# Softmax attention with maxima from the leading halves, four heads at once in row quarters, and one denominator product a head group

## The reference

```python
def _L1_xattn_ref(x, context, w_q, b_q, w_k, b_k, w_v, b_v, w_o, b_o):
    q = x @ w_q + b_q
    k = context @ w_k + b_k
    v = context @ w_v + b_v
    # reshaped to (B, 512, 16 heads, 32)
    scores = jnp.einsum('bqhd,bkhd->bhqk', q, k) * scale
    weights = jax.nn.softmax(scores, axis=-1)
    out = jnp.einsum('bhqk,bkhd->bqhd', weights, v).reshape(B, Lq, D)
    return out @ w_o + b_o
# x = x + _L1_xattn_ref(layernorm(x), ctx, ...)
```

## Time and profile before

| | us |
|---|---|
| median of three runs | 1724.04 |
| lowest, highest | 1719.91, 1727.51 |
| span of the profiled execution | 1727.3 |
| of it, softmax attention, first projection to last output | 629.7 to 1436.5 |
| one batch of it in the middle (905.1 to 999.6) | 94.5 |

### The profile page before, as it was taken

The page is one execution under the profiler, slowest core; times in us unless marked ns, Lnnn a source line. Parts: engine busy times, 40 slices in busy tenths (PEclk is TensorE's granted clock), DMA queues, the critical chain, the costliest instruction groups (busy, mean ns, idle before and its releaser), DMA issues. The chain is left out here.

```text
span 1727.3 us, 29488 instructions
## 1 busy us (share of the span) xinstructions
PE 1589.8 (92%) x8932; PEld 719.8 (42%) x8932; DVE 1226.5 (71%) x1756; ACT 1150.9 (67%) x1895; POOL 1022.9 (59%) x738
## 2 busy tenths in 40 slices
PE   5999878998999977899999999999999978999998
PEld 3545433443444432334444444444443423444443
DVE  4978898997888745676776767676767665665553
ACT  5667599787888744665757666666657567556662
POOL 4776436765678723565657666665756665455452
PEclk9989999999999997999999999999999989999999
DMA  8421000000000122121211212121211200010001
GB/s 309 146 73 32 1 1 1 1 1 1 0 1 1 45 59 81 32 58 25 58 34 36 56 27 57 27 55 32 58 25 40 55 22 28 25 49 24 24 24 49
DMA packets 60463, 72.22 MB, mean 42 GB/s; under 512 B 14416, under 2 KB 40016, under 8 KB 59856
## 3 DMA queue, kind: packets, MB, share of 16 engines
q1 hardware_dynamic: 56944, 62.22, 12.3%
q10 hardware_dynamic: 3424, 8.91, 1.3%
HBM read 37.40 MB, written 8.39 MB: 27 GB/s over the span
## 5 line engine op out<-in xcount | busy, mean ns | idle before, releaser
L1556 DVE TENSOR_REDUCE s_mx<-bank 128x1 f32<-128x512 f32 x512 | 337.3, 685 | 199.8 <-PE bank L1684 193.7
L1443 ACT ACTIVATE s_E<-bank 128x512 f32<-128x512 f32 x512 | 293.9, 595 | 202.5 <-PE bank L1698 177.2
L1342 POOL TENSOR_TENSOR s_E<-s_E 128x1024 f32<-128x1024 f32 x128 | 300.5, 2367 | 125.4 <-PE bank L1706 117.9
L1684 PE MATMUL bank<-s_KA,s_QA 96*128 96x512 f16 x512 | 194.2, 390 | 17.7 <-DMA s_KA<-sm_cx 7.1
L1698 PE MATMUL bank<-s_QA,s_KA 97*128 97x512 f16 x512 | 196.7, 386 | 3.8 <-DMA s_QA<-s_mrow 1.4
L1335 POOL TENSOR_TENSOR sm_cx<-s_qkf,sm_cx 128x512 f16<-128x512 f32 x64 | 76.5, 1195 | 175.6 <-ACT sm_cx L1421 175.4
L1867 POOL TENSOR_TENSOR sm_cx<-m_xf,sm_cx 128x512 f16<-128x512 f32 x60 | 84.1, 1408 | 104.9 <-ACT sm_cx L1909 104.9
L1706 PE MATMUL bank<-s_E,s_V 128*32 128x512 f32 x1024 | 135.6, 602 | 4.3 <-ACT s_E L1443 4.3
L1075 PE MATMUL bank<-sm_zz,w1raw 128*128 128x512 f16 x256 | 100.3, 392 | 31.1 <-DVE sm_cx L962 16.3
L1098 PE MATMUL bank<-f_w2q,w2raw 128*128 128x512 f16 x512 | 122.2, 380 | 0.4 <-ACT w2raw L912 0.4
L772 POOL TENSOR_TENSOR sm_wkv<-sm_wkv,sm_cx 128x511 f32<-128x511 f32 x48 | 66.1, 1378 | 94.2 <-DVE sm_wkv L962 94.1
(11 more groups left out here) (264 smaller groups left out, 4092.1 us busy)
## 6 DMA issues: line engine op xcount, KB each, us to landing
sm_cx<-in_ctx SPq DMA_DIRECT2D x16, 768.0 KB, 4.6
s_QA<-sm_cx SPq DMA_DIRECT2D x384, 32.0 KB, 1.9
s_KA<-sm_cx SPq DMA_DIRECT2D x372, 32.0 KB, 1.9
X<-in_x SPq DMA_DIRECT2D x8, 1024.0 KB, 6.8
out_x<-X SPq DMA_DIRECT2D x8, 1024.0 KB, 4.3
w1raw<-in_w ACTq DMA_DIRECT2D x1, 4096.0 KB, 14.2
w2raw<-in_w ACTq DMA_DIRECT2D x1, 4096.0 KB, 28.7
w1raw<-in_wq SPq DMA_DIRECT2D x1, 1024.0 KB, 5.1
```

Of the source, the lines that this page charges most:

```text
L1342: e.tensor_tensor(into, into, other, ALU.add).then_inc(s_sum.sem, 1)
L1443: e.activation(E[:, SLOT[k] + h, :], SC[u % 2][:, :], ACT.Exp, scale=1.0 / float(np.sqrt(DH)))\
L1556: e.tensor_reduce(mx[:, q, h:h + 1], MX[q % 2][:, :], AX.X, ALU.max).then_inc(s_red.sem, 1)
L1684: e.matmul(MX[k % 2][:, :], QA[0:MROW, m, h, q * P:(q + 1) * P], KA[0:MROW, m, h, :], start=True, stop=True).then_inc(s_mx.sem, 1)
```

## The change

The rest of the kernel is as before; in `softmax_attention` this is different:

- Maxima multiply only the high halves of queries and keys, straight from qkh (now double-buffered) without the stack: 32 rows a head, the four heads in the four row quarters of the array, into four banks. VectorE reduces four banks in one instruction, and one transpose of 16 columns replaces four. The exact scores keep their stacked operands; the row subtracted from them cancels in the division.
- The exponentials of all four key tiles are added up before one product with ones: five additions on GpSimd and one on VectorE a group (key tile 3, heads 2 and 3), instead of four on GpSimd and two products. The product goes to the bank of the numerators (ND), after these were copied, and the inverse into SBUF (RD). It stands in unit 3 of the next step.
- PSUM is dealt out anew: SC two banks, MX four, ND one, R one. Queries, keys, values and outputs all go through R.
- The output product is spread over m = 0 (four pieces), 1 (eight) and 2 (four). The normalising moves from VectorE to ScalarE, with two small instructions on GpSimd (`centre`). QA and KA have three slots for four.
- The units of all work are dealt out anew, and all programs are written out, without loops.

The tables and bank numbers:

```diff
-    NSH = 12
-    SPARSE_K, SPARSE_V = (-1, 1, 3), (5, 7, 9, 12)
-    K_UNITS = (SPARSE_K, (-1, 0, 1), (2, 3, 4), SPARSE_K)
-    V_UNITS = (SPARSE_V, (12, 13, 14, 15), SPARSE_V, SPARSE_V)
-    T_UNITS, STATS_UNITS = (4, 6, 8, 10), (1, 3, 6, 10)
-    OUTPUT = {1: ((0, 0),), 2: ((0, 1),), 3: ((0, 2), (0, 3)), 5: ((1, 0),), 6: ((1, 1),), 7: ((1, 2), (1, 3)),
-              9: ((2, 0),), 10: ((2, 1),), 11: ((2, 2), (2, 3)), 13: ((3, 0),), 14: ((3, 1),), 15: ((3, 2), (3, 3))}
-    RESIDUAL = {4: 0, 8: 1, 12: 2}
-    A_UNIT, A_LATE = UNITS - 1, 6
+    nc, X, tile, banks, psum, ident, ones = (env[k] for k in ("nc", "X", "tile", "banks", "psum", "ident", "ones"))
+
+    UNITS, G, NSH, NSLOT = 4 * TT, NG * B, 12, 3
+    Q_UNITS = ((0, 1, 2, 3), (0, 1, 2, 3), (4, 4, 5, 5), (0, 1, 2, 3))
+    K_UNITS = ((4, 5, 6), (4, 4, 5), (7, 8, 8), (4, 5, 6))
+    V_UNITS = ((8, 8, 9, 9), (9, 9, 10, 10), (12, 12, 13, 13), (8, 9, 11, 12))
+    PV_UNITS = ((7, 10, 14), (7, 10, 14), (9, 12, 15), (7, 10, 14))
+    OUTPUT = ({11: ((0, 0),), 12: ((0, 1),), 13: ((0, 2),), 15: ((0, 3),)},
+              {6: ((1, 0), (1, 1)), 8: ((1, 2), (1, 3)), 11: ((2, 0), (2, 1)), 12: ((2, 2), (2, 3))},
+              {0: ((3, 0), (3, 1)), 1: ((3, 2), (3, 3))}, {})
+    ROWS_UNIT, DN_UNIT, T_UNITS = (13, 13, 14, 13), 3, (13, 13, 13, 15)
+    DIV_UNIT, DIV_LATE = (10, None, 15, 12), 5
+    NORM_UNITS = (2, 4, 5, 6)
```

```diff
-        SC, MX, NUM, DEN, R6, R7 = banks[0:2], banks[2:4], banks[4], banks[5], banks[6], banks[7]
+        SC, MX, ND, R = (0, 1), (2, 3, 4, 5), 6, 7
+        four = psum[:, MX[0] * S:(MX[0] + 4) * S].rearrange("p (h s) -> p h s", s=S)
```

TensorE, the changed operations and the order of a step:

```diff
+            def maxima(g, q):
+                if q == 0:
+                    e.wait_ge(s_qkh, 2 * g + 2)
+                need(e, s_red, 4 * g + q)
+                for i in MX:
+                    take(i)
+                for h in range(4):
+                    rows = slice(h * DH, (h + 1) * DH)
+                    last = e.matmul(banks[MX[h]][:, :], qkh[rows, g % 2, 0, q * P:(q + 1) * P], qkh[rows, g % 2, 1, :],
+                                    start=True, stop=True)
+                last.then_inc(s_mx, 1)
+
+            def rows(g):
+                e.wait_ge(s_red, 4 * g + 4)
+                e.transpose(banks[MX[0]][0:4 * TT, 0:P], mx[:, g % 2, :, :].rearrange("p h q -> p (h q)"), ident[:, :])\
+                    .then_inc(s_mT, 1)
+                reader[MX[0]] = (s_mrow, g + 1)
+
...
+            def denominators(g):
+                e.wait_ge(s_av, g + 1)
+                e.wait_ge(s_sum, 5 * g + 5)
+                e.wait_ge(s_sumv, g + 1)
                 for h in range(4):
-                    e.matmul(DEN[h * DH:(h + 1) * DH, :], ones[:, 0:DH], E[:, SLOT[2 * p] + h, :], start=(p == 0), stop=(p == 1))\
-                        .then_inc(s_dn.sem, 1)
-
-            def transposed(b, c, end=False):
+                    last = e.matmul(banks[ND][h * DH:(h + 1) * DH, :], ones[:, 0:DH], E[:, slot(g, 0) + h, :],
+                                    start=True, stop=True)
+                last.then_inc(s_dn, 1)
+
```

```diff
+            def step(b, m, g, proj, nxt, div):
+                last = b == B - 1
+                if nxt:
+                    maxima(nxt, 0 if m == 2 else 1)
+                if div is not None:
+                    attend(div, TT - 1)
                 for u in range(UNITS):
...
+                    score(g, u)
+                    if b:
+                        for q, c in OUTPUT[m].get(u, ()):
+                            if m == 2:
+                                output(b - 1, q, c)
+                    if proj:
+                        for c in range(KD):
+                            if u == Q_UNITS[m][c]:
+                                queries(proj, 0, c)
+                    if u == DN_UNIT:
+                        if m == 2 and nxt:
+                            maxima(nxt, 1)
+                        if div is not None:
+                            denominators(div)
+                    if proj:
+                        for c in range(KC):
+                            if u == K_UNITS[m][c]:
+                                queries(proj, 1, c)
+                    if u in PV_UNITS[m]:
+                        t = PV_UNITS[m].index(u)
+                        if nxt and t < 2:
+                            maxima(nxt, t + 2)
+                        if proj and t == 2 and m != 1:
+                            maxima(proj, 0)
+                        attend(g, t)
+                    if proj:
+                        for t in range(TT):
+                            if u == V_UNITS[m][t]:
+                                values(proj, t)
+                    if b and m != 2:
+                        for q, c in OUTPUT[m].get(u, ()):
                             output(b - 1, q, c)
...
+                    if nxt and u == ROWS_UNIT[m]:
+                        rows(nxt)
+                    if m == 1:
+                        for c in range(KD):
+                            if u == T_UNITS[c]:
+                                transposed(b + 1, c, MX[(c + 1) % 4])
```

GpSimd (`summed(g, t, i)` adds key tile t of two heads to the running sum in the slot of tile 0; s_sum reaches 5g + 5 with the last one of group g):

```diff
+            def summed(g, t, i):
+
+                into, other = (E[:, slot(g, k) + 2 * i:slot(g, k) + 2 * i + 2, :] for k in (0, t))
+                if t == 1:
+                    e.wait_ge(s_pv, 4 * g + 1)
+                else:
+                    e.wait_ge(s_sum, 5 * g + 2 * (t - 2) + i + 1)
+                e.wait_ge(s_ex, 16 * g + 4 * t + 2 * i + 2)
+                e.tensor_tensor(into, into, other, ALU.add).then_inc(s_sum, 1)
...
+            def step(b, m, g, proj, nxt, div):
+                last = b == B - 1
+                if div is not None:
+                    summed(div, 3, 0)
+                if m == 2 and proj:
+                    context(b + 1)
...
+                if proj:
+                    low(proj, 0)
+                e.tensor_tensor(tile(b, m), tile(b, m), bo[:, :], ALU.add).then_inc(s_bo, 1)
                 if last and m == 3:
                     mixed(0)
-                    mixed(1)
+                if proj:
+                    low(proj, 1)
                 if m == 2:
-                    divided(b, 0)
-                e.tensor_tensor(tile(b, m), tile(b, m), bo[:, :], ALU.add).then_inc(s_bo.sem, 1)
+                    divided(4 * b)
+                summed(g, 1, 0)
+                if m == 0 and div is not None:
+                    divided(div)
+                summed(g, 1, 1)
                 if m == 0:
                     ln_p(e, b + 1)
...
+                if last and m == 3:
+                    mixed(1)
+                summed(g, 2, 0)
+                if m == 3 or m == 2:
+                    divided(div)
+                summed(g, 2, 1)
```

ScalarE, what the exponentials wait for, and the order of a step:

```diff
+            def exponential(g, u):
+
+                t, h = divmod(u, 4)
+                if t == 0:
+                    need(e, s_pv, 4 * (g - 1) + 3)
+                    need(e, s_sum, 5 * (g - 1) + 3 + h // 2 if g else 0)
+                if t == 1:
+                    need(e, s_pv, 4 * g)
+                    need(e, *((s_sumv, g) if h // 2 else (s_sum, 5 * g)))
+                if t == 2:
+                    need(e, s_dn, g)
+                if t == 3:
+                    e.wait_ge(s_pv, 4 * g + 2)
+                    e.wait_ge(s_sum, 5 * g + 1 + h // 2)
+                e.wait_ge(s_sc, 16 * g + u + 1)
+                e.activation(E[:, slot(g, t) + h, :], banks[SC[u % 2]][:, :], ACT.Exp, scale=1.0 / float(np.sqrt(DH)))\
+                    .then_inc(s_ex, 1)
...
+            def step(b, m, g, proj, nxt, div):
+                last = b == B - 1
+                if div is not None:
+                    numerators(div)
...
+                    if m == 2 and not last and u in (1, 2, 3):
+                        context(b + 1, u - 1)
+                    exponential(g, u)
+                    if m == 1:
+                        for c in range(KD):
+                            if u == min(T_UNITS[c] + 1, UNITS - 1):
+                                if last:
+                                    shifted(c, MX[(c + 1) % 4])
+                                else:
+                                    high(b + 1, c, MX[(c + 1) % 4])
...
+                    if m == 1 and u in NORM_UNITS:
+                        normalised(b + 1, NORM_UNITS.index(u))
+                    if proj and u == Q_UNITS[m][-1] + 1:
+                        queries(proj, 0)
                     if proj and u == K_UNITS[m][-1] + 1:
-                        queries(*proj, 1)
...
+                    if proj and u == V_UNITS[m][-1] + 1:
+                        values(proj)
+                    if m == 2 and u == DIV_LATE:
+                        divided(4 * b)
+                    if div is not None and u == DIV_UNIT[m]:
+                        divided(div)
+                    if nxt and u == min(ROWS_UNIT[m] + 1, UNITS - 1):
+                        rows(nxt)
```

(44 more changed lines are left out.)

655 lines of the change are left out of this document (262 added, 393 removed).

## The result

The changed kernel takes 1893.66 us (median; 1892.52 to 1894.52), the kernel before, with one run more than ahead of the prediction, 1724.97 (1719.91 to 1727.51): a ratio of 1.098, 95% interval 1.096 to 1.101. It is 9.8% slower. The forecast was 1835, with a range up to 1890: the direction and the order of size are right, and the time lies just above the range.

A forecast was written before the change was run, and what follows sets the result against it. TensorE bounds the kernel before; the changed one a loop through GpSimd's sums, 111.7 us a batch for 94.4. Over 7.5 batches 130, less 13 for the first and last, less 7.5 at the beginning: 1835 us, range 1690 to 1890.

The forecast's parts named there:

- The price of a set of maxima: TensorE: four matmuls on row quarters work at once, 0.3 us a set with the change of form.
- the serial rival: TensorE's row quarters run one after another, 1.0 us a set, +40 us; chance 0.08 together with a falling clock.
- The price of VectorE's sum: VectorE's sixth sum, 1024 columns: 1.22 us, interpolated between 512 and 2048 columns.
- the turns: VectorE's and GpSimd's adds take turns at SBUF, so the sixth sum's 1.22 us comes after the fifth.
- The steps by the loop: Denominator product to product through four engines: steps of 23.0, 26.0, 34.6 and 28.1 us, 111.7 a batch for 94.4.
- the last link of the loop: On TensorE, the denominator product waits for all six sums, then takes 0.97 us and 0.1 of signals.
- the walk: Count of each step from one denominator product's end to the next, through TensorE, ScalarE, GpSimd and VectorE; 111.7 us a batch.
- the forecast's case: The loop through GpSimd's sums sets the steps, TensorE partly idle: 1835 us, own range 1790 to 1870, chance 0.47.
- Bank R: Queries, keys, values and outputs share one bank, each waiting until its predecessor was read: 1.3, 1.3, 6.0 and 1.1 us.
- Beginning, end, unrolling: Around the stage's steps: beginning 7.5 us less (0 to 12), end 0, unrolling of TensorE, SyncE and GpSimd 0.
- Engines' loads decide: Rival: each step costs its fullest engine, 80.4 us a batch; about 1670 with half the gain lost to waits; chance 0.22.
- The rival of clock and serial quarters: Row quarters run serially (+40 us) or TensorE's clock falls (1 to 3 us a light step): 1870 to 1890; chance 0.08.

The follow-up runs named there:

- combo7: combo2 with GpSimd's fifth sum moved to VectorE at its own step's end, behind the first outputs' residual; 1774.9 us.
- short: Changed kernel with GpSimd's last three sums of a group cut to 32 columns a head instead of 512; 1889.7 us.
- combo2: mx_late plus earlier ScalarE reads of queries, keys, values and the row of maxima, with divided pairs, low halves, output bias and first outputs reordered; 1785.6 us.
- mx_late: Changed kernel with the next group's first maxima set moved from the step's end to behind an attend at the next step's start; 1861.4 us.
- warm: Changed kernel with TensorE's idle time filled by repeats of the next score's matmul, 7 a step, results thrown away; 1876.3 us.
- pairs: mx_late with maxima taken two heads at a time in two banks, keys and values given banks of their own, outputs alternating; 1905.7 us.

## Why the prediction was right, and where it was wrong

**The price of a set of maxima: right.** The four matmuls start together and the next instruction starts 0.33 us later (TensorE in order of time):

```profile
1006.64 0.39 PE L1711 MATMUL bank<-s_qkh 32*128 32x512 f16 x4
1006.97 1.06 PE L1736 MATMUL bank<-s_E,s_V 128*32 128x512 f32 x8
1007.96 0.39 PE L1728 MATMUL bank<-s_QA,s_KA 97*128 97x512 f16 x1
```

0.3 was taken, the serial rival said 1.0. The attend takes the 0.97 of the denominators and 0.02 more. TensorE's work fell from 93.9 to about 83 us a batch; the forecast said 14 us less, the trace shows some 11, an estimate from the stretch above. combo7's batch, nearly at full clock, bears it out with 83.8 us busy.

**The price of VectorE's sum: right alone, and the turns are there.** VectorE's sum in three kernels: unedited, short, combo2 (count, total, mean ns):

```profile
L1565 DVE TENSOR_TENSOR s_E<-s_E 128x1024 f32<-128x1024 f32 x32 | 48.3, 1508 | 13.1 <-POOL s_E L1321 6.8 <-ACT s_E L1445 6.3
```
```profile
L1565 DVE TENSOR_TENSOR s_E<-s_E 128x1024 f32<-128x1024 f32 x32 | 39.0, 1218 | 7.0 <-POOL s_E L1321 7.0
```
```profile
L1567 DVE TENSOR_TENSOR s_E<-s_E 128x1024 f32<-128x1024 f32 x32 | 84.6, 2643 | 37.7 <-POOL s_E L1321 37.3
```

With GpSimd's sums shortened it is 1.22 us, the value interpolated. In the unedited kernel it overlaps GpSimd's work in 10 of 32 turns (mean 1.51), in combo2 in 24 (2.64). The forecast's 1.22 was near, but the turn cost nothing here, since the denominators did not wait for it.

**The steps by the loop: near in size, wrong in what ends them. This is the step that failed.** The forecast counted from product to product. The denominators' products in the trace, steps m=0, 1, 2, 3 and 0 again:

```profile
1001.20 1.06 PE L1745 MATMUL bank<-s_E,ones 128*32 128x512 f32 x8
...
1027.99 1.07 PE L1745 MATMUL bank<-s_E,ones 128*32 128x512 f32 x8
...
1065.48 1.06 PE L1745 MATMUL bank<-s_E,ones 128*32 128x512 f32 x8
...
1096.36 1.06 PE L1745 MATMUL bank<-s_E,ones 128*32 128x512 f32 x8
...
1120.77 1.06 PE L1745 MATMUL bank<-s_E,ones 128*32 128x512 f32 x8
```

They give 26.8, 37.5, 30.9 and 24.4 us for a forecast of 26.0, 34.6, 28.1 and 23.0: 0.8, 2.9, 2.8 and 1.4 too little, 7.9 a batch, 59 us over 7.5 batches. (The terms listed up to exponential 14 in m=1 add to 21.9, not 22.9; 1.0 of that step has no term.) The walk through GpSimd was good: in the step from m=3 into m=0 its second low half starts 6.7 us after the product's end, as forecast, and the fifth sum is through at 20.5, for 20.6. GpSimd and VectorE there, and TensorE in the same step:

```profile
1104.05 1.15 POOL L1311 TENSOR_TENSOR sm_cx<-s_qkf,s_qkh 128x512 f16<-128x512 f32 x1 [1.20 <-ACT s_qkh L1422]
1105.16 6.97 POOL L1321 TENSOR_TENSOR s_E<-s_E 128x1024 f32<-128x1024 f32 x3
1112.09 1.16 POOL L1326 TENSOR_TENSOR s_atl<-s_AT,s_ath 128x512 f16<-128x512 f32 x1
1113.21 4.65 POOL L1321 TENSOR_TENSOR s_E<-s_E 128x1024 f32<-128x1024 f32 x2
1117.29 1.65 DVE L1565 TENSOR_TENSOR s_E<-s_E 128x1024 f32<-128x1024 f32 x1
```
```profile
1111.27 0.62 PE L1711 MATMUL bank<-s_qkh 32*128 32x512 f16 x4 [2.62 <-ACT s_mrow L1464]
1111.82 1.94 PE L1736 MATMUL bank<-s_E,s_V 128*32 128x512 f32 x8
```

The last sum ends at 1118.94, and the product starts at 1120.77, 1.8 us later, without a wait of its own: TensorE was not there. It had waited 2.62 us for the row's copy and then run at the low clock. In the steps shown the product comes 0.9, 2.9, 2.6 and 1.8 us behind the last sum. What failed is the last link of the loop, the product's wait for the sums: TensorE's own queue comes there later, by waits and by a low clock that the walk had put at nothing. Between the row's copy and the product in the steps m=2 and m=3 (us, TensorE's busy time, granted clock):

```profile
1086.12:1096.36 10.24, 9.25 (x40) 0.63 0.09 23
1110.88:1120.77 9.89, 9.34 (x41) 0.66 0.37 93
```

The row's copy in m=2 starts 19.7 us after the product's end (the walk had 19.9), the next product 10.2 us after it (the walk 7.2). By the busy share times what 0.63 and 0.66 lack to 1, the low clock stretched TensorE's work there by 3.4 and 3.2 us, an estimate; either is more than the margin between sums and product. That GpSimd's sums stand straight behind a low half was right in m=0, 2 and 3; in m=1 the first one, at 1040.77, follows an attend. I had followed the sums to the product and not asked whether TensorE would be there first.

**What it left out.** Two things make TensorE the later one, and both were half seen.
- The row of maxima in m=2 was followed to the next step's scores (by its copy), not to its bank. That bank is also written by the maxima queued at the end of the step, with two attends behind. mx_late priced this order, with the wait for VectorE's low half at the same place: 6.3 us a batch, 32 us. With it the products come on average only 0.2 to 0.7 us behind the last sum, and over 700 to 1400 us they wait 7.9 us for it: the loop then stands directly behind.
- The fallen clock was a rival of its own at 0.08, with 1 to 3 us for a light step. It came together with the forecast's case: the forecast expected TensorE to be partly idle, and the earlier trace rows shows the clock at half after such a stretch. About 10 us of stretch a batch, by the estimate above; warm got 2.7 us a batch back, net of its fill. That the miss of 7.9 a batch is smaller than the two together is no contradiction, since a part of each is time in which TensorE would have waited for the sums; how it divides is not shown. Behind the measurement: the Trainium skill ("TensorE: Matmul & The Clock Gate", Why this matters for your kernels) warns of idle gaps on TensorE for this reason; the trace agrees, with 0.89 in this batch where the kernel before has 1.00.

**Bank R: right.** The walk had 1.3, 1.3, 6.0 and 1.1 us of waits, 9.7 a batch; in the batch shown they are 8.3 for queries and keys, 1.2 for values, 0.6 for a residual: 10.1. pairs confirms those of m=1.

**Beginning, end, unrolling.** From the first product to the first row of maxima 11.1 us less; 7.5 was taken, of 0 to 12. Besides, the stage started 10.1 us earlier. Its start lies between 618.6 and 627.1 us in all edits of the changed kernel and at 629.6 and 629.7 in the two of the kernel before. Nothing ahead of the stage is in the diff but the one tensor that holds the eight banks; the cause stays open. The end cost 4 us for a forecast of 0. The first and last batches were to be 13 us shorter than the others; between the first and last rows of maxima the stage took 182.7 us more for a forecast of 117, so 59 of the 66 missed lie in the steps and 7 in those batches. That the whole comes out 59 us over the forecast as well is chance: the 7 and the end's 4 nearly cancel the earlier start and the 3.6 more at the beginning. Unrolling: 0, as told.

**The rivals.** "Engines' loads decide" failed: no engine is busy for more than 78% of the batch, and the steps still take 24.8 to 35.8 us where this rival had 17.1 to 23.4. The rival of clock and serial quarters named 1870 to 1890, the nearest number, with one of its two mechanisms right; its chance should have been added to the forecast's case and not set beside it.

## What to carry to other kernels

When a saving leaves the bounding engine partly idle, ask for each instruction in its queue what it must wait for and what stands behind it: an early instruction that needs a late buffer holds up all that needs nothing. A loop through another engine binds only if it arrives last where it closes, so walk the bounding engine's own queue to that place too; and cut the loop in an experiment at the place that it passes, since a cut ahead of a wait for something else tells nothing. And price the lower clock into every case in which TensorE is to become less busy.

## What the runs showed of the hardware

- Four fp16 matmuls of 512 columns on quarters of the rows took 0.33 us with the change of form, where one on all rows takes 0.22.
- An add of 1024 columns on VectorE took 2.64 us on average in combo2, where it overlapped GpSimd's adds in 24 of 32 turns, and 1.22 in short, where it did so in 2.
- Discarded matmuls in TensorE's gaps made the kernel 17 us faster (warm), as the granted clock rose from 0.925 to 0.952.
- A reciprocal of 512 columns from a bank took VectorE 3.35 us, for four of 128 columns at 0.93 each before; it is the longest item in its queue in a step of the unedited kernel.
